# Attention loop of a fused transformer block: masked-query transposes moved to the first gap, attended transpose ahead of the weighted values, projection moved to the values' bank

## Chip, cores and metric

The kernel runs on 1 core of one Trainium2 chip. The metric is device time in microseconds of one execution, the median of the runs.

## What is computed

Two blocks follow each other on x of 16 sequences x 128 tokens x 128 features, all float32. The change touches the first, a conditioned transformer block:

```python
mod = (c @ ada_w.T + ada_b)[:, None, :]
sh_msa, sc_msa, g_msa, sh_mlp, sc_mlp, g_mlp = jnp.split(mod, 6, axis=-1)
h = modulate(rmsnorm(x, norm1_w), sh_msa, sc_msa)
qkv = (h @ qkv_w.T).reshape(B, N, 3, H, D)      # H = 16 heads of D = 8
q, k = rmsnorm of each head, then rotary positions
attn = softmax(einsum('bnhd,bmhd->bhnm', q, k) * D ** -0.5)
o = einsum('bhnm,bmhd->bnhd', attn, v).reshape(B, N, C)
x = x + g_msa * (o @ proj_w.T + proj_b)
ff = silu(h2 @ w1.T) * (h2 @ w3.T) @ w2.T       # h2 from x as h above
x = x + g_mlp * ff
```

(The two lines on q and k are abridged.) The second block is linear attention with two layer norms; it is not touched.

## The kernel before

Every engine runs its own instruction stream, written out by hand, and waits on semaphores; the order of the calls in each stream is the order of the work. All matrix results go to eight banks of PSUM of 128 partitions x 512 float32. The work runs one sequence at a time. After a prologue that loads and transposes weights, a loop of LAST_A = 18 iterations (line 2014 for TensorE, 1447 for ScalarE, 1729 for VectorE, 1227 for GpSimd) runs as a pipeline in which iteration t works on several sequences at once:

- TensorE `round_(t, 0)` and `round_(t, 1)` (lines 1862 to 1890) are two half rounds. Each has 4 matmuls of raw scores of sequence t + 2 (line 1878, to banks 0 and 1), from which VectorE takes the row maxima (`rowmax`, line 1601), and 8 of transposed scores of sequence t that have the maxima folded in (line 1887, to banks 2 and 3), which ScalarE exponentiates (`exp`, line 1302). The second half round waits for the maxima and the exponentials of the first, since it writes the same banks. VectorE seeds a reciprocal square root for two sequences at a time (`square_sums`, `seeds`, lines 1658 to 1673) in iterations of odd t.
- `projection(t - 2)` (line 1898) multiplies the attended values of sequence t - 2 by the output weights, to columns 384:512 of bank 5. VectorE multiplies that by the gate (x1g, line 1648) and adds the input (x1, line 1651), both in `after_attention`.
- `token_major(t - 1)` (line 1906) transposes the value sums of sequence t - 1, which ScalarE copied out of bank 6 (`summed`, line 1371), back into the other half of bank 6. From there VectorE takes the reciprocals (line 1612) and the product o (`attended`, line 1620).
- `queries_and_keys(t + 3)` (line 1911) transposes padded queries and keys to bank 4; VectorE spreads them (`keys_apart`, `queries`, lines 1630 and 1638). GpSimd made them (`normed`, line 1192) out of rotated and normed heads; it also adds a bias to the input (`input_biased`, line 1224), for which x1 waits.
- `input_turned(t + 6)` (line 1933) and `queries_keys_values(t + 6)` (line 1940) are the input transpose and the product to queries, keys and values of a later sequence; ScalarE makes the modulated input between them (line 1319) and copies behind them (lines 1336, 1344, 1355). Both end at t = 9.
- `queries_and_max(t + 1)` (line 1948, helper line 1911) transposes the queries that carry their row maximum as a ninth element, the masked queries, to columns 0:256 of bank 5; ScalarE copies them to qTm (line 1328), which the next half rounds read.
- `weighted_values(t, 0)` and `(t, 1)` (line 1965) are 8 small matmuls each over the exponentials, to columns 0:256 of bank 6. From t = B - 6 = 10 on, the first of them stands ahead of the masked-query transposes and the second behind.
- `attended(t - 1)` (line 1977) transposes o of sequence t - 1 to bank 5, and ScalarE copies it (line 1363) for the projection one iteration later.

The profile records a float32 matmul as two rows' worth of instructions and a transpose as one.

From t = 14 on, parts of the feed-forward block (`b_first`, `b_input`, `b_rest`, lines 863 to 875) are dealt into the iterations. At t = 10 to 13 TensorE prepares biases and centred weights in them, and VectorE has the style vectors (lines 1564 to 1568) at the end of t = 8. Behind the loop come the rest of the feed-forward block and the second block.

## Time and profile before

| | |
|---|---|
| median of 3 runs | 210.18 us (210.06, 210.18, 211.2) |
| span of the profiled execution | 208.4 us (its own time is not given apart from this) |
| TensorE matmul busy | 183.2 us (88%) |
| TensorE weight load busy | 143.4 us (69%) |
| VectorE busy | 165.3 us (79%) |
| ScalarE busy | 130.1 us (62%) |
| GpSimd busy | 140.7 us (67%) |
| attention loop, t = 0 to 15 | 29.3 to 128.9 us of the span |
| granted TensorE clock | full (2.4 GHz) in every slice |

The span goes from the first to the last recorded instruction of one execution; the runs are timed from outside and have a little more. Busy times are sums over instructions that can overlap on TensorE. In the rows further down, a start time is counted from the start of the span, and brackets give the idle time of the engine before the row with what released it.

### The profile page before, as it was taken

How to read it: one execution, taken by the hardware profiler on the slowest of the kernel's cores; microseconds unless marked ns; L12 is line 12 of the kernel's file. 1: busy time of each engine (PE TensorE's matmuls, PEld its weight loads, DVE VectorE, ACT ScalarE, POOL GpSimd, SP SyncE). 2: the span in 40 equal slices, each digit the busy share in tenths (PEclk: the TensorE clock that was granted, in tenths of full speed). 3: DMA queues.
4: the chain of work that ended last, by engine and by line, in shares of the span. 5: the costliest groups of instructions: out<-in, count | busy, mean ns of one | idle time of the engine just before them, and what ended most of it. 6: DMA issues, size and time to landing. Idle time of an engine off the chain costs nothing.

```text
span 208.4 us, 6070 instructions
## 1 busy us (share of the span) xinstructions
PE 183.2 (88%) x2039; PEld 143.4 (69%) x2039; DVE 165.3 (79%) x498; ACT 130.1 (62%) x377; POOL 140.7 (67%) x333
## 2 busy tenths in 40 slices
PE   2598887999899999898899899899998899999963
PEld 1355556677687777776677676799997677888642
DVE  6699898895979889996785615768889788999882
ACT  1367797666777777675545775445343367999741
POOL 8889798999888887958900583416443746768651
PEclk9999999999999999999999999999999999999999
DMA  6962007700000000000000000000000000000111
GB/s 113 282 207 113 0 9 288 318 2 3 3 3 2 6 3 0 3 0 5 3 0 3 3 0 2 3 0 2 5 0 0 2 3 0 0 28 28 50 50 53
DMA packets 10428, 8.32 MB, mean 40 GB/s; under 512 B 3105, under 2 KB 9886, under 8 KB 9886
## 3 DMA queue, kind: packets, MB, share of 16 engines
q1 hardware_dynamic: 7006, 7.25, 10.3%
q10 hardware_dynamic: 3392, 0.68, 1.6%
q8 instruction: 17, 0.28, 0.6%
q14 instruction: 13, 0.11, 0.2%
HBM read 6.86 MB, written 1.07 MB: 38 GB/s over the span
## 4 chain that ended last, share of the span: by engine, by line
PE 46%; DVE 16%; issue 6%; ACT 4%; POOL 3%; POOLq 0%; ACTq 0%; DVEq 0%
DVE qkpad L1601 6%; PE bank L1887 6%; PE bank L1965 5%; PE bank L1878 5%; PE bank L875 5%; PE bank L863 5%; PE bank L864 4%; PE bank L992 2%; PE bank L1940 2%; PE bank L908 2%; ACT probs L1302 1%; PE bank L1977 1%; PE bank L1911 1%; PE bank L972 1%; PE bank L1898 1%
## 5 line engine op out<-in xcount | busy, mean ns | idle before, releaser
L1601 DVE TENSOR_REDUCE qkpad<-bank 128x4 f32<-128x512 f32 x64 | 41.0, 683 | 12.1 <-PE bank L1878 11.0
L1302 ACT ACTIVATE probs<-bank 128x512 f32<-128x512 f32 x64 | 34.7, 594 | 22.3 <-PE bank L1887 22.3
L1887 PE MATMUL bank<-qTm,kBD 32*128 32x128 f32 x512 | 37.1, 283 | 0.4 <-ACT probs L1302 0.4
L1878 PE MATMUL bank<-kBD,qTs 32*128 32x256 f32 x224 | 31.8, 398 | 4.8 <-DVE qkpad L1601 3.7
L1887 PEld LDWEIGHTS bank<-qTm,kBD 32*128 32x128 f32 x512 | 31.0, 186 | 1.0 <-ACT probs L1302 0.6
L1878 PEld LDWEIGHTS bank<-kBD,qTs 32*128 32x128 f32 x224 | 20.0, 184 | 9.8 <-DVE qkpad L1601 6.6
L1965 PE MATMUL bank<-probs,vpad 128*32 128x128 f32 x512 | 18.5, 276 | 2.8 <-ACT probs L1302 1.6
L575 ACT ACTIVATE th<-bank 128x256 f32<-128x256 f32 x24 | 9.2, 383 | 18.7 <-PE bank L864 15.3
L1965 PEld LDWEIGHTS bank<-probs,vpad 128*32 128x32 f32 x512 | 12.8, 109 | 6.8 <-issue 3.1
L1911 PE MATMUL bank<-ident,qkpad 128*128 128x128 f32 x96 | 16.3, 279 | 0.4 <-POOL qkpad L1192 0.2
L1130 POOL TENSOR_TENSOR partner<-qk,rope 128x96 f32<-128x96 f32 x32 | 14.4, 470 | 3.2 <-ACT qk L1344 3.2
L1940 PE MATMUL bank<-qkvT,hT 128*128 128x384 f32 x32 | 15.3, 571 | 0.5 <-ACT hT L1319 0.5
L1911 PEld LDWEIGHTS bank<-ident,qkpad 128*128 128x128 f32 x96 | 11.2, 141 | 6.2 <-issue 3.1
L505 POOL TENSOR_TENSOR x<-fg,x 128x256 f32<-128x256 f32 x6 | 4.4, 727 | 15.5 <-DVE fg L691 15.5
L863 PE MATMUL bank<-hT,w1T 128*128 128x256 f32 x48 | 14.5, 384 | 0.0
L864 PE MATMUL bank<-hT,w3T 128*128 128x256 f32 x48 | 14.3, 379 | 0.0
L674 DVE SCALAR_TENSOR_TENSOR yg<-th,bank 128x256 f32<-128x256 f32 x24 | 10.0, 419 | 4.1 <-ACT th L575 4.1
L875 PE MATMUL bank<-w2T,ff 128*128 128x128 f32 x96 | 13.2, 275 | 0.0
L515 POOL TENSOR_TENSOR rstd<-var,minus_half 128x2 f32<-128x2 f32 (+1 forms) x17 | 11.7, 689 | 1.4
L875 PEld LDWEIGHTS bank<-w2T,ff 128*128 128x128 f32 x96 | 12.4, 191 | 0.4
L1141 POOL TENSOR_TENSOR rot<-qk,rope 128x256 f32<-128x256 f32 x16 | 11.7, 728 | 0.0
L1192 POOL TENSOR_TENSOR qkpad<-rot,ny 128x256 f32<-128x256 f32 x15 | 9.7, 647 | 2.2 <-DVE ny L1691 0.4
(253 smaller groups left out, 518.4 us busy)
## 6 DMA issues: line engine op xcount, KB each, us to landing
gate<-in_cond_dram SPq DMA_DIRECT2D x1, 1024.0 KB, 4.4
x<-gate_rows SPq DMA_DIRECT2D x1, 1024.0 KB, 4.6
y<-gate_rows SPq DMA_DIRECT2D x1, 1024.0 KB, 6.7
res<-gate_rows SPq DMA_DIRECT2D x1, 1024.0 KB, 10.1
out_dram<-res SPq DMA_DIRECT2D x7, 128.0 KB, 1.8
xin<-in_x_dram ACTq DMA_DIRECT2D x2, 256.0 KB, 5.3
xin<-in_x_dram SPq DMA_DIRECT2D x1, 512.0 KB, 5.0
ada_n<-in_L_cond_ada_w_dram SPq DMA_DIRECT2D x1, 256.0 KB, 5.3
```

Source lines behind the costliest of these rows:

```text
L515: q.tensor_tensor(rstd[:, rows], var[:, rows], minus_half[:, 0:rows.stop - rows.start], ALU.pow).then_inc(made, 1)
L863: q.matmul(bank[GU_BANK[c]][:, 0:UNIT * T], w1T[:, c * 128:c * 128 + 128], flat(hT2[1 - p]), start=True, stop=True)
L864: q.matmul(bank[GU_BANK[c]][:, UNIT * T:], w3T[:, c * 128:c * 128 + 128], flat(hT2[1 - p]), start=True, stop=True).then_inc(b_gu, 1)
L875: last = q.matmul(bank[F_BANK[j]][:, 0:D], ff[c][:, j * T:(j + 1) * T], w2T[:, c, :], start=c == 0, stop=c == FC - 1)
L1130: last = q.tensor_tensor(heads(partner[b % 2][:, :, :])[:, :, :, k::2], heads(qk[b % NQK][:, :, :])[:, :, :, 1 - k:ROPE:2], table(b, 1)[:, ...
L1302: q.activation(probs[2 * r + i][:, :, :, :].rearrange("p f a t -> p (f a t)"), bank[E_BANK[i]][:, :], ACT.Exp, scale=SCALE).then_inc(s_p, 1)
L1601: q.tensor_reduce(out_, score_bank(b, r, i)[:, :].rearrange("p (f a t) -> p f a t", f=2, a=2), X_AXIS, ALU.max, negate=True).then_inc(s_ma ...
L1878: last = q.matmul(bank[S_BANK[i]][:, f * 2 * T:(f + 1) * 2 * T], qTs[b % 2][rows, f, :], kBD[b % NKB][rows, f, :, :].rearrange("p a t -> p ...
L1887: last = q.matmul(bank[E_BANK[i]][:, (2 * f + k) * T:(2 * f + k + 1) * T], kBD[t % NKB][rows, f, k, :], qTm[t % 2][rows, f, :], start=True ...
L1911: last = q.transpose(dst[:, at_ + f * T:at_ + (f + 1) * T], qkpad[b % NKB][:, s, 8 * f:8 * f + 8, :].rearrange("p h d -> p (h d)"), ident[ ...
L1940: q.matmul(front_bank(b)[:, 128:512], hT[b % 2][:, :], qkvT[:, :], start=True, stop=True).then_inc(s_qkv, 1)
L1965: last = q.matmul(bank[O_BANK][32 * c:32 * c + 32, r * T:(r + 1) * T], vpad[b % NVP][:, col:col + VSTEP], probs[2 * r + i][:, f, k, :], st ...
```

## The change

Three things move, and the waits follow them. On TensorE the masked-query transposes of iteration t go from the stretch behind the second half round to the stretch behind the first, ahead of the queries and keys; ScalarE's copy of them goes ahead of the modulated input. The transpose of o goes from behind the weighted values to ahead of them (for t < B), and ScalarE's copy of it ahead of the squares; for t >= B - 6 the first weighted values no longer stand ahead of the masked queries. The projection writes columns 0:128 of bank 6, the values' bank, in place of bank 5. So it waits for the copy of the value sums, VectorE's gate multiplication waits for the transposes in that bank, and the next weighted values wait for the gate multiplication. On VectorE the reciprocals, the gate multiplication (now `gated_projection`) and o come right behind the first maxima, and the addition to x1 behind the second maxima.

```diff
@@ -957,5 +957,5 @@
                     e.wait_ge(c_hT, u + 1)
                     if u == 0:
-                        e.wait_ge(s_on, B)
+                        e.wait_ge(s_x1g, B)
                         e.wait_ge(pv_v, V_DONE)
                     wait(e, c_kx, u)
@@ -1454,13 +1454,16 @@
                 if t >= B - 2:
                     b_input(t - B, t % 2)
+                queries_and_max(t + 1)
                 modulated_input(t + 6)
                 exp(t, 1, 0)
                 exp(t, 1, 1)
-                queries_and_max(t + 1)
+                if t < B:
+                    attended(t - 1)
                 squares(t + 6)
                 queries_keys(t + 6)
                 if t >= B - 1:
                     b_rest(t - B)
-                attended(t - 1)
+                if t >= B:
+                    attended(t - 1)
                 summed(t)
                 values(t + 6)
@@ -1639,12 +1642,19 @@
                                 ALU.mult).then_inc(s_kq, 1)
 
-            def after_attention(b):
+            def gated_projection(b):
 
                 if not is_seq(b):
                     return
                 v.wait_ge(s_proj, b + 1)
+                v.wait_ge(s_oq, min(b + 2, B))
+                wait(v, s_x1, b)
                 if b == 0:
                     v.wait_ge(ld_g1, 16)
-                q.tensor_tensor(x1g[:, :], bank[P_BANK][:, 384:512], g1_rows[:, b, :], ALU.mult).then_inc(s_x1g, 1)
+                q.tensor_tensor(x1g[:, :], bank[O_BANK][:, 0:D], g1_rows[:, b, :], ALU.mult).then_inc(s_x1g, 1)
+
+            def after_attention(b):
+
+                if not is_seq(b):
+                    return
                 v.wait_ge(s_x1g, b + 1)
                 v.wait_ge(s_xb, b + 1)
@@ -1730,16 +1740,14 @@
                 rowmax(t + 2, 0, 0)
                 rowmax(t + 2, 0, 1)
-                if t < B:
-                    after_attention(t - 2)
                 reciprocals(t - 1)
+                gated_projection(t - 2)
+                attended(t - 1)
                 keys_apart(t + 3)
                 queries(t + 3)
-                attended(t - 1)
                 if t == B - 1:
                     b_first(t - B)
-                if t >= B:
-                    after_attention(t - 2)
                 rowmax(t + 2, 1, 0)
                 rowmax(t + 2, 1, 1)
+                after_attention(t - 2)
                 square_sums(t + 6)
                 seeds(t + 6)
@@ -1895,6 +1903,7 @@
                     return
                 e.wait_ge(s_oT, b + 1)
+                e.wait_ge(s_oT4, min(b + 2, B))
                 wait(e, s_x1g, b)
-                q.matmul(bank[P_BANK][:, 384:512], oT[:, :], projT[:, :], start=True, stop=True).then_inc(s_proj, 1)
+                q.matmul(bank[O_BANK][:, 0:D], oT[:, :], projT[:, :], start=True, stop=True).then_inc(s_proj, 1)
 
             def token_major(b):
@@ -1945,5 +1954,5 @@
                     return
                 e.wait_ge(s_max, NC * (b + 1))
-                wait(e, s_x1g, b - 2)
+                wait(e, s_oT, b - 2)
                 halves(bank[P_BANK], 0, b, 0).then_inc(s_tp, 1)
 
@@ -1956,4 +1965,5 @@
                     e.wait_ge(s_v, max(b + 1, FRONT_B))
                     wait(e, s_on, b)
+                    wait(e, s_x1g, b - 1)
                     if b == 0:
                         e.wait_ge(pv_a, A_ROWS)
@@ -1973,6 +1983,4 @@
                 e.wait_ge(s_on, b + 1)
                 wait(e, s_qTm, min(b + 3, B))
-                if b >= B - 2:
-                    e.wait_ge(s_x1g, b)
                 q.transpose(bank[P_BANK][:, 256:384], o[:, :, :].rearrange("p h d -> p (h d)"), ident[:, :]).then_inc(s_oTp, 1)
 
@@ -2014,11 +2022,14 @@
             for t in range(LAST_A):
                 round_(t, 0)
+                projection(t - 2)
+                token_major(t - 1)
                 if t == B - 1:
                     b_first(t - B, t % 2)
                     b_input(t - B, t % 2)
-                projection(t - 2)
-                token_major(t - 1)
                 if t >= B:
                     b_first(t - B, t % 2)
+                if t == 0:
+                    e.wait_ge(pv_a, A_DONE)
+                queries_and_max(t + 1)
                 queries_and_keys(t + 3)
                 input_turned(t + 6)
@@ -2031,11 +2042,7 @@
                 round_(t, 1)
                 queries_keys_values(t + 6)
-                if t >= B - 6:
-                    weighted_values(t, 0)
-                if t == 0:
-                    e.wait_ge(pv_a, A_DONE)
-                queries_and_max(t + 1)
-                if t < B - 6:
-                    weighted_values(t, 0)
+                if t < B:
+                    attended(t - 1)
+                weighted_values(t, 0)
                 if t == B - 1:
                     b_rest(t - B, t % 2)
@@ -2044,5 +2051,5 @@
                     b_input(t - B, t % 2)
                     b_rest(t - B, t % 2)
-                attended(t - 1)
+                    attended(t - 1)
             blocks_tensor(e, 2)
 
```

How this moves TensorE's instructions. Names are destination<-sources; each f32 matmul counts once here; `ident` marks a transpose. Before, iteration t = 3, from the end of the first half round (projection of line 1898, value transposes 1906, queries and keys 1911, input 1933):

```order
L1898 MATMUL bank<-projT,oT 128x128 [waits s_x1g,s_oT]
L1906 MATMUL bank<-ident,oT 128x128 [waits s_oT4]
L1906 MATMUL bank<-ident,oT 128x128
L1911 MATMUL bank<-ident,qkpad 128x128 [waits s_kq,s_nm]
L1911 MATMUL bank<-ident,qkpad 128x128 x3
L1933 MATMUL bank<-ident,xs 128x128 [waits s_v,s_xs]
```

and from the end of its second half round (1940 queries-keys-values, 1911 with s_x1g and s_max the masked queries, 1965 weighted values, 1977 transpose of o):

```order
L1911 MATMUL bank<-ident,qkpad 128x128 [waits s_x1g,s_max]
L1911 MATMUL bank<-ident,qkpad 128x128
L1965 MATMUL bank<-probs,vpad 32x128 [waits s_on,s_v,s_p]
L1965 MATMUL bank<-probs,vpad 32x128 x7
L1965 MATMUL bank<-probs,vpad 32x128 [waits s_p]
L1965 MATMUL bank<-probs,vpad 32x128 x7
L1977 MATMUL bank<-ident,o 128x128 [waits s_qTm,s_on]
```

The change, the same iteration (every line number is higher here; 1907 is the projection, 1915 the value transposes, 1920 the masked queries first and then queries and keys):

```order
L1907 MATMUL bank<-projT,oT 128x128 [waits s_x1g,s_oT4,s_oT]
L1915 MATMUL bank<-ident,oT 128x128 [waits s_oT4]
L1915 MATMUL bank<-ident,oT 128x128
L1920 MATMUL bank<-ident,qkpad 128x128 [waits s_oT,s_max]
L1920 MATMUL bank<-ident,qkpad 128x128
L1920 MATMUL bank<-ident,qkpad 128x128 [waits s_kq,s_nm]
L1920 MATMUL bank<-ident,qkpad 128x128 x3
L1942 MATMUL bank<-ident,xs 128x128 [waits s_v,s_xs]
```

and behind the second half round (1949 queries-keys-values, 1985 transpose of o, 1975 weighted values):

```order
L1949 MATMUL bank<-qkvT,hT 128x384 [waits s_hT]
L1985 MATMUL bank<-ident,o 128x128 [waits s_qTm,s_on]
L1975 MATMUL bank<-probs,vpad 32x128 [waits s_on,s_x1g,s_v,s_p]
L1975 MATMUL bank<-probs,vpad 32x128 x7
L1975 MATMUL bank<-probs,vpad 32x128 [waits s_p]
L1975 MATMUL bank<-probs,vpad 32x128 x7
L1886 MATMUL bank<-kBD,qTs 128x256 [waits s_qTm,s_p,s_max,s_kq]
```

The masked-query pair has gone into the upper stretch, the transpose of o stands ahead of the values, and the projection has a wait for s_oT4, the copy of the value sums, in the place where it stood.

VectorE in the same iteration, before, from the gate multiplication on (1648 x1g, 1651 x1, 1612 reciprocals, 1630 and 1638 keys and queries spread, 1620 o, 1601 second maxima, 1658 square sums):

```order
L1648 TENSOR_TENSOR x1g<-bank,x 128x128 [waits s_proj]
L1651 TENSOR_TENSOR x<-x1g,xin 128x128 [waits s_xb,s_x1g]
L1612 RECIPROCAL rsum<-bank 128x16 [waits s_oq]
L1630 TENSOR_TENSOR kBD<-bank,pmask 128x512 [waits s_e1,s_e0,s_tq]
L1638 TENSOR_SCALAR qTs<-bank,rowmask 128x256
L1620 TENSOR_TENSOR o<-bank,rsum 128x128 [waits s_oTp,s_rec]
L1601 TENSOR_REDUCE qkpad<-bank 128x2x2 [waits s_s0]
L1601 TENSOR_REDUCE qkpad<-bank 128x2x2 [waits s_s1]
L1658 TENSOR_REDUCE nms<-sq 128x32 [waits s_sq]
```

and with the change (1615 reciprocals, 1653 x1g, 1623 o, 1633 and 1641 keys and queries, 1604 second maxima, 1661 x1, 1668 square sums):

```order
L1615 RECIPROCAL rsum<-bank 128x16 [waits s_oq]
L1653 TENSOR_TENSOR x1g<-bank,x 128x128 [waits s_x1,s_oq,s_proj]
L1623 TENSOR_TENSOR o<-bank,rsum 128x128 [waits s_oTp,s_rec]
L1633 TENSOR_TENSOR kBD<-bank,pmask 128x512 [waits s_e1,s_e0,s_tq]
L1641 TENSOR_SCALAR qTs<-bank,rowmask 128x256
L1604 TENSOR_REDUCE qkpad<-bank 128x2x2 [waits s_s0]
L1604 TENSOR_REDUCE qkpad<-bank 128x2x2 [waits s_s1]
L1661 TENSOR_TENSOR x<-x1g,xin 128x128 [waits s_xb,s_x1g]
L1668 TENSOR_REDUCE nms<-sq 128x32 [waits s_sq]
```

o has moved from fifth to third place behind the first maxima, and x1 from ahead of the second maxima to behind them. GpSimd's and SyncE's orders are as before.

## Rows read from the trace of the kernel before

**Rows 1.** Waits of TensorE, whole span: total us, times, longest us.

```profile
PE bank L1878 <- DVE qkpad L1601: 3.7, 9, 1.3
...
PE bank L1898 <- ACT oT L1363: 0.9, 2, 0.5
```

**Rows 2.** Timeline, TensorE, iteration t = 8: start us, us, engine, line, operation.

```profile
78.44 0.48 PE L1878 MATMUL bank<-kBD,qTs 32*128 32x256 f32 x2
...
79.55 0.49 PE L1898 MATMUL bank<-projT,oT 128*128 128x128 f32 x2
79.87 0.38 PE L1906 MATMUL bank<-ident,oT 128*128 128x128 f32 x2
80.09 0.60 PE L1911 MATMUL bank<-ident,qkpad 128*128 128x128 f32 x4
...
81.00 0.48 PE L1878 MATMUL bank<-kBD,qTs 32*128 32x256 f32 x2 [0.20 <-DVE qkpad L1601]
...
82.85 0.38 PE L1911 MATMUL bank<-ident,qkpad 128*128 128x128 f32 x2
83.16 1.08 PE L1965 MATMUL bank<-probs,vpad 128*32 128x128 f32 x32
84.17 0.33 PE L1977 MATMUL bank<-ident,o 128*128 128x128 f32 x1
84.43 0.48 PE L1878 MATMUL bank<-kBD,qTs 32*128 32x256 f32 x2
```

**Rows 3.** Timeline, VectorE, t = 7 to 8.

```profile
79.27 0.20 DVE L1673 TENSOR_SCALAR ny<-nms 128x64 int32<-128x64 int32 x1
79.61 1.29 DVE L1601 TENSOR_REDUCE qkpad<-bank 128x4 f32<-128x512 f32 x2
...
81.13 0.42 DVE L1651 TENSOR_TENSOR x<-x1g,xin 128x128 f32<-128x128 f32 x1
81.47 0.24 DVE L1612 RECIPROCAL rsum<-bank 128x16 f32<-128x16 f32 x1
...
82.77 1.28 DVE L1601 TENSOR_REDUCE qkpad<-bank 128x4 f32<-128x512 f32 x2
```

**Rows 4.** Windows: length, busy us of PE, PEld, DVE, ACT, POOL; clock; DMA.

```profile
50.44:56.98 6.54, 5.86 (x95) 4.57 (x95) 5.63 (x14) 4.62 (x14) 6.04 (x15) 1.00 0.01 3
56.98:87.55 30.57, 29.02 (x471) 22.70 (x471) 27.29 (x66) 22.74 (x66) 25.94 (x63) 1.00 0.01 3
93.59:97.43 3.84, 3.06 (x60) 2.13 (x60) 2.96 (x8) 1.47 (x3) 3.23 (x9) 1.00 0.02 4
99.96:103.71 3.75, 3.02 (x62) 2.11 (x60) 2.95 (x8) 1.47 (x3) 3.26 (x8) 1.00 0.02 4
107.07:110.32 3.25, 2.94 (x60) 2.07 (x59) 2.20 (x5) 1.36 (x3) 0.00 (x0) 1.00 0.00 0
112.88:116.10 3.22, 2.95 (x59) 2.07 (x60) 2.90 (x10) 1.36 (x3) 0.00 (x0) 1.00 0.00 0
118.47:121.63 3.16, 2.93 (x51) 2.06 (x51) 0.86 (x3) 2.01 (x5) 2.85 (x6) 1.00 0.00 0
124.44:129.36 4.92, 4.55 (x58) 3.33 (x57) 3.23 (x10) 2.71 (x8) 2.45 (x5) 1.00 0.00 2
```

**Rows 5.** Timeline, ScalarE, t = 8.

```profile
78.72 0.38 ACT L1371 ACTIVATE oT<-bank 128x256 f32<-128x256 f32 x1
...
82.25 1.08 ACT L1302 ACTIVATE probs<-bank 128x512 f32<-128x512 f32 x2 [0.95 <-PE bank L1887]
```

**Rows 6.** Timeline, TensorE, queries and keys of t = 3.

```profile
49.74 0.66 PE L1911 MATMUL bank<-ident,qkpad 128*128 128x128 f32 x4 [0.24 <-POOL qkpad L1192]
```

**Rows 7.** Timeline, TensorE, weighted values of t = 3, 10 and 12.

```profile
53.16 1.08 PE L1965 MATMUL bank<-probs,vpad 128*32 128x128 f32 x32 [0.48 <-DVE o L1620]
...
95.53 0.64 PE L1965 MATMUL bank<-probs,vpad 128*32 128x128 f32 x16 [0.76 <-ACT probs L1302]
...
109.49 0.64 PE L1965 MATMUL bank<-probs,vpad 128*32 128x128 f32 x16 [0.30 <-ACT probs L1302]
```

More of the change, by code:

```diff
@@ L1644, in after_attention @@
                     return
-                v.wait_ge(s_proj, b + 1)
-                if b == 0:
-                    v.wait_ge(ld_g1, 16)
-                q.tensor_tensor(x1g[:, :], bank[P_BANK][:, 384:512], g1_rows[:, b, :], ALU.mult).then_inc(s_x1g, 1)
                 v.wait_ge(s_x1g, b + 1)
```

3 lines of the change are left out of this document (added).

## Prediction

> **What bounds the kernel now.** I read four views, in this order. The waits of TensorE come first: what did it stand still for? It waited for VectorE's row maxima nine times, 3.7 us in all, and twice for ScalarE before a projection, up to 0.5 us [rows 1]. The timeline of TensorE in one iteration of the attention loop, t = 8, comes second [rows 2]. The reader is to see two stretches. The first goes from the first half round (78.44) to the second (81.00), 2.56 us, and ends with 0.20 us of idle time released by the row maxima. The second goes from there to the next iteration (84.43), 3.43 us, with no idle time at all. Third, VectorE in the same iteration [rows 3]: the two maxima start at 79.61, end at 80.90, and the second half round follows 0.1 us later, so the first stretch is a chain (scores, maxima, scores) and not TensorE's own work. Last, windows of the loop [rows 4]: from the second half round of t = 4 to that of t = 9 TensorE is busy 29.02 of 30.57 us. So the first stretch is set by a chain through VectorE, the second by TensorE's instruction stream. Work that leaves the second and fits under the chain of the first is time saved.
>
> **Steady iterations, t = 4 to 9.** The pair of masked-query transposes moves from the second stretch to the first. Where it stands now it costs 83.16 - 82.85 = 0.31 us; the value transposes, the same kind of pair with transposes behind it, cost 80.09 - 79.87 = 0.22 us [rows 2]. The first stretch has 0.20 us idle, so a pair of 0.22 us fits to within 0.02: I take 2.56 us unchanged. Its bounds are 0 and +0.11 us (0.31 - 0.20). The transpose of the attended values goes ahead of the weighted values; it costs 84.43 - 84.17 = 0.26 us last in the stretch, and I expect 0.2 to 0.26 in its new place. The second stretch becomes 3.43 - 0.31 - 0.02 = 3.10 us. For that the weighted values must not wait: their first half needs exponentials of the first half round and the attended product o, which VectorE now makes third after the maxima instead of fifth, a microsecond earlier.
>
> ScalarE's moved copies cost nothing: the copy of the masked queries (0.38) goes into idle time of 0.95 us ahead of the exponentials [rows 5], and the copy of the attended values takes the place it left. If that cover were gone, TensorE would wait for the modulated input in front of the queries-keys-values product.
>
> VectorE sets the pace of every odd iteration, in which it also seeds the Newton steps. At t = 7 the seeds end at 79.47 and the maxima start at 79.61 [rows 3]: about 0.1 us of slack, in a period of 5.99. The change moves the addition to x1 (a step of 81.47 - 81.13 = 0.34) from before the second maxima to behind them. Its scores are there by then (1.1 us after the half round, against maxima that start at 1.77), so the maxima start 0.34 earlier and the seeds come out when they did. The sum of VectorE's steps is the same, but for a dependent pair (x1g, x1) that is pulled apart, perhaps 0.05. I take 5.85 us for an odd period and 2.56 + 3.10 = 5.66 for an even one, 0.47 less than 11.98 for a pair. From the second half round of t = 4 to that of t = 9 the window has 30.57 us [rows 4]: two pairs and one even period whose end the style work on VectorE sets. I get 5.66 + 5.85 + 5.66 + 5.85 + 6.50 = 29.52: **-1.05 us**.
>
> **Iterations 0 to 3.** At t = 3 TensorE waits 0.24 us for GpSimd's normed keys [rows 6], and GpSimd works without a pause until there. Whatever the first three iterations gain ends in that wait: **0 us** (were GpSimd not in the way, it would be 3 times 0.31). Behind it the gain begins: the weighted values of t = 3 wait 0.48 us for o [rows 7], since o stands behind x1, which waits for GpSimd. In the new order o no longer stands behind it. The window of 6.54 us from the second half round of t = 3 to that of t = 4 [rows 4] becomes an odd period like the others, 5.85: **-0.69 us**.
>
> **Iterations 10 to 14.** There is no projection to queries, keys and values any more. The first weighted values wait for o (0.76 us at t = 10, and about as long at t = 11; the view names ScalarE, whose exponentials end with o), and the transposes stand between the two halves of the values [rows 7]. In the new order the first half starts at once and the second waits for the last exponentials, 2.42 us after the half round (109.49 - 107.07). With 0.57 of values behind it the second stretch is 3.0 us. It is 3.84, 3.75, 3.25, 3.22 and 3.16 us at t = 10 to 14 [rows 4]; the last, which has 0.1 less in front of its values' wait, I take at 2.9. That saves 0.84 + 0.75 + 0.25 + 0.22 + 0.26 = 2.32 us. The second stretch of t = 9 saves 0.33 like the others. The first stretches pay 0.22 us for the moved pair at t = 10, 11 and 12, 0.1 at t = 13, where 0.1 is idle, and nothing at t = 14, where they wait for exponentials: 0.76. Together **-1.89 us**.
>
> **The last two iterations.** The attended transpose of t = 15 now comes ahead of 2 us of feed-forward work, +0.2; the projection behind it no longer waits for its copy but for the copy of the value sums, which was the next thing on ScalarE. 4.92 us [rows 4] become about 5.0: **+0.1**. Behind that, the same instructions run in the same order.
>
> **The sum.** -1.05 - 0.69 - 1.89 + 0.1 = -3.5 us. That is the end at which each piece finds its place with no new wait. The other end has 0.11 more in each first stretch from t = 4 on (ten of them, +1.1) and odd periods of 5.9 instead of 5.85 (+0.1): -2.3 us. Nothing in the rows favours either, so I take the middle, -2.9. The profiled execution has a span of 208.4 us; the median of the runs, 210.18, is 1.8 above it for what lies around the span, which the change leaves alone. So 205.5 for the span and **207.3 us** for the median. A difference of 0.5% (1.05 us) is about what a measurement of this kernel can tell from none.
>
> **A rule against the change.** The projection now writes the bank that already holds the value sums and their transposes. The rows show that the turns fit today: the copy of the sums starts at 78.72 and ends at 79.10 [rows 5], and the projection starts at 79.55 [rows 2]. The Trainium skill (PSUM — Partial Sum Buffer, section PSUM bank collisions raise a hardware error) says that accesses of different engines to one bank have to be kept apart by semaphores whatever their address. By that rule every user of this bank now takes turns, and if the turns were the bound the result would be that of the third rival below, 211.9 instead of 207.3. The rows above do not show such a bound.
>
> **Rivals.**
> *TensorE alone is the bound.* The moved pair costs the same wherever it stands, and only the shown idle time is to be had: 0.20 us in the six iterations 4 to 9, 1.2 us, while from t = 10 on the last exponentials give the pace as before. 209.0 us. For it: 29.02 busy of 30.57. Against it: the waits for o at t = 3, 10 and 11 are idle time of TensorE as well.
> *VectorE is the bound in odd iterations and gives the gain back.* If x1 ahead of the seeds is not paid for by earlier maxima, the seeds and the next maxima come 0.34 us late in three odd iterations (+1.0), and iteration 3 gains only half (+0.3): 2.9 - 1.3 = 1.6 us less than before, 208.6. For it: 0.1 us of slack. Against it: x1 leaves the path to the maxima by as much as it enters behind them.
> *The bank's turns block TensorE: slower.* The projection now waits for ScalarE's copy of the sums of the iteration before, and behind it stand the value transposes, the masked queries, the keys and the next half round. If it stood there 0.5 us, the longest wait in front of a projection [rows 1], each first stretch would grow by 0.45 and each second shrink by 0.33: +0.12 in 14 iterations, +1.7, **211.9 us**. It decides once the copy ends 1.5 us after the start of an iteration; it ends at 0.66 now. ScalarE has to run 0.8 us late, and nothing in its rows says so.
> *The change does less than it says:* the second stretch is refilled by ScalarE's last exponentials in every iteration. They end at 82.25 + 1.08 = 83.33, and the second half of the values would start at about 83.6: not before 0.2 us more is cut. 0 to 1 us of gain, 209.7.
>
> **How the numbers follow.** The forecast (206.4 to 208.2) has 0.68, and a gain above it 0.06; TensorE alone 0.08, VectorE 0.10, the refilled stretch 0.04, the turns 0.04. The rivals at 208.6 and 209.0 are faster by over 0.5% (the border is 209.13), the second only just. Faster: 0.68 + 0.06 + most of 0.18, less a little for waits nobody named, 0.83; same: 0.13; slower: 0.04. The range is 206.3 to 209.2: it takes in both ends of the sum, the gain of 3.5 and some more, and the first two rivals; beyond it lie the last two and the best case.
>
> **What would show it.** In the new profile, the first stretch of t = 8 should be 2.5 to 2.65 us with the maxima or nothing as releaser, the second 3.1; the idle time of TensorE before the second half round should be near 0 in even iterations and 0.1 to 0.2 in odd ones. GpSimd's keys should cost TensorE more than 0.24 us at t = 3 (some 0.7). The waits for o should be gone and waits for exponentials of 0.3 to 0.9 us should stand before the second values from t = 10 on. A wait for ScalarE before a projection of the loop, or periods of 6.0 in odd iterations, would prove me wrong.

## The result, and the profile of the changed kernel

| | before | changed |
|---|---|---|
| median of the runs | 210.12 us (4 runs) | 207.34 us (207.23 to 207.52, 4 runs) |
| ratio | | 0.9853, 95% interval 0.9829 to 0.9877 |
| span of the profiled execution | 208.4 us | 205.4 us |
| TensorE matmul busy | 183.2 us | 180.9 us |

Predicted were 207.3 and a span of 205.5. The interval of the ratio stays clear of 1, so the change makes the kernel 1.5% faster. The size is right; its parts are less so.

TensorE's waits in the changed kernel (total us, times, longest us), against [rows 1]. Line 1886 is the raw scores (1878 before), 1920 masked queries, queries and keys (1911), 1975 the weighted values (1965), 1907 the projection (1898).

```profile
PE bank L1886 <- DVE qkpad L1604: 3.4, 5, 1.2
...
PE bank L1975 <- ACT probs L1302: 2.0, 5, 0.5
...
PE bank L1920 <- POOL qkpad L1192: 1.1, 1, 1.1
...
PE bank L1907 <- ACT oT L1363: 0.5, 1, 0.5
```

The maxima release it five times instead of nine, but for almost as long in all; the exponentials hold the second half of the values five times (t = 10 to 14); GpSimd's keys hold it once, at t = 3, for 1.1 us instead of 0.24 [rows 6].

TensorE, t = 8, against [rows 2]:

```profile
76.86 0.48 PE L1886 MATMUL bank<-kBD,qTs 32*128 32x256 f32 x2
...
78.29 0.38 PE L1915 MATMUL bank<-ident,oT 128*128 128x128 f32 x2
78.51 0.82 PE L1920 MATMUL bank<-ident,qkpad 128*128 128x128 f32 x6
79.17 0.27 PE L1942 MATMUL bank<-ident,xs 128*128 128x128 f32 x1
79.53 0.48 PE L1886 MATMUL bank<-kBD,qTs 32*128 32x256 f32 x2
...
80.64 0.91 PE L1949 MATMUL bank<-qkvT,hT 128*128 128x384 f32 x2
81.39 0.27 PE L1985 MATMUL bank<-ident,o 128*128 128x128 f32 x1
81.59 1.08 PE L1975 MATMUL bank<-probs,vpad 128*32 128x128 f32 x32
82.60 0.48 PE L1886 MATMUL bank<-kBD,qTs 32*128 32x256 f32 x2
```

The six transposes stand together, and the second stretch is 82.60 - 79.53 = 3.07 us (3.43 before). VectorE around it, against [rows 3]; 1661 is the addition to x1, 1623 o:

```profile
64.66 0.83 DVE L1661 TENSOR_TENSOR x<-x1g,xin 128x128 f32<-128x128 f32 x1
...
78.19 1.28 DVE L1604 TENSOR_REDUCE qkpad<-bank 128x4 f32<-128x512 f32 x2
...
79.70 0.28 DVE L1623 TENSOR_TENSOR o<-bank,rsum 128x128 f32<-128x128 f32 x1
...
82.08 0.70 DVE L1661 TENSOR_TENSOR x<-x1g,xin 128x128 f32<-128x128 f32 x1
...
88.95 0.27 DVE L1661 TENSOR_TENSOR x<-x1g,xin 128x128 f32<-128x128 f32 x1
```

o starts 1.5 us after the first maxima. The three rows of line 1661 are t = 5, 8 and 9: the addition, behind the second maxima now, takes 0.83, 0.70 and 0.27 us for the same tile. Before, it took 0.65, 0.42 and 0.33 us in these iterations.

Windows, as in [rows 4]: from the second half round of t = 3 to that of t = 4, on to that of t = 9, and second stretches of t = 10 and 12.

```profile
50.45:56.53 6.08, 5.64 (x95) 4.45 (x94) 5.89 (x12) 4.80 (x14) 5.79 (x14) 1.00 0.01 3
56.53:86.39 29.86, 28.16 (x470) 22.32 (x470) 28.00 (x66) 22.03 (x66) 26.30 (x64) 1.00 0.01 3
92.29:95.28 2.99, 2.58 (x58) 1.87 (x58) 2.91 (x6) 1.25 (x3) 2.36 (x9) 1.00 0.03 8
...
104.68:107.67 2.99, 2.58 (x58) 1.87 (x57) 1.85 (x4) 1.25 (x3) 0.00 (x0) 1.00 0.03 5
```

| piece | before | changed | difference | predicted |
|---|---|---|---|---|
| to the second half round of t = 3 | 50.44 | 50.45 | 0.0 | 0 |
| to that of t = 4 | 6.54 | 6.08 | -0.46 | -0.69 |
| to that of t = 9 | 30.57 | 29.86 | -0.71 | -1.05 |
| to the projection of sequence 14 | 41.81 | 40.01 | -1.80 | -1.89 + 0.1 |
| to the end of the span | 79.0 | 79.0 | 0.0 | 0 |

Inside the fourth piece one second stretch is not like the others: that of t = 11 is 101.10 - 97.84 = 3.26 us, where t = 10 and 12 have 2.99.
Its raw scores begin and end like this, with a bias matmul (line 1843) among them:

```profile
97.84 0.48 PE L1886 MATMUL bank<-kBD,qTs 32*128 32x256 f32 x1
...
98.00 0.37 PE L1843 MATMUL bank<-bqv,ones 1*128 1x256 f32 x1
...
98.86 0.37 PE L1886 MATMUL bank<-kBD,qTs 32*128 32x256 f32 x1
```

### The profile page after: what moved, and what is told of

It is laid out like the page before. It is cut to its first block, busy times and chain, and to the rows that moved or that the text cites. A ratio compares the mean times of both kernels' runs of the same rounds, so it can differ in the third digit from the quotient of the medians.

```text
span 205.4 us, 6100 instructions
## 1 busy us (share of the span) xinstructions
PE 180.9 (88%) x2039; PEld 142.3 (69%) x2039; DVE 166.1 (81%) x498; ACT 129.4 (63%) x377; POOL 141.3 (69%) x333
## 3 DMA queue, kind: packets, MB, share of 16 engines
HBM read 6.86 MB, written 1.07 MB: 39 GB/s over the span
## 4 chain that ended last, share of the span: by engine, by line
PE 40%; DVE 17%; issue 8%; POOL 5%; ACT 4%; POOLq 0%; ACTq 0%; DVEq 0%
PE bank L1895 5%; DVE qkpad L1604 5%; PE bank L875 5%; PE bank L1886 5%; PE bank L863 5%; PE bank L864 4%; PE bank L1975 4%; ACT probs L1302 2%; PE bank L908 2%; POOL rstd L515 2%; PE bank L1907 1%; PE bank L1920 1%; PE bank L992 1%; PE bank L1949 1%; PE bank L972 1%
## 5 line engine op out<-in xcount | busy, mean ns | idle before, releaser
L1130 POOL TENSOR_TENSOR partner<-qk,rope 128x96 f32<-128x96 f32 x32 | 14.4, 471 | 2.0 <-ACT qk L1344 2.0
L1920 PE MATMUL bank<-ident,qkpad 128*128 128x128 f32 x96 | 14.2, 277 | 1.4 <-POOL qkpad L1192 1.1
L863 PE MATMUL bank<-hT,w1T 128*128 128x256 f32 x48 | 14.4, 382 | 0.0
```

The costliest lines, as they stand in the source:

```text
L863: q.matmul(bank[GU_BANK[c]][:, 0:UNIT * T], w1T[:, c * 128:c * 128 + 128], flat(hT2[1 - p]), start=True, stop=True)
L1130: last = q.tensor_tensor(heads(partner[b % 2][:, :, :])[:, :, :, k::2], heads(qk[b % NQK][:, :, :])[:, :, :, 1 - k:ROPE:2], table(b, 1)[:, ...
L1920: last = q.transpose(dst[:, at_ + f * T:at_ + (f + 1) * T], qkpad[b % NKB][:, s, 8 * f:8 * f + 8, :].rearrange("p h d -> p (h d)"), ident[ ...
```

## The experiments

The loop starts at 29.1 to 30.2 us in these profiles, whatever the kernel. In two of them (e5, e9) the granted clock was lower for a while after the loop, and in that of e7 on the kernel before it was lower ahead of the loop (0.50 in the window from 20 to 22 us). So beside the medians stands the **loop time**: from TensorE's first raw scores of t = 0 to its last projection, the one behind a 0.53 us wait. Before: 134.87 - 29.34 = 105.53 us; changed: 131.87 - 29.18 = 102.69. The medians of before that were taken beside the runs below lay between 210.18 and 210.59.

| kernel | median | loop time | against the changed kernel's loop |
|---|---|---|---|
| before | 210.12 | 105.53 | +2.84 |
| changed | 207.34 | 102.69 | |
| e1 TensorE's and ScalarE's orders back | 209.66 | 104.23 | +1.54 |
| e2 transpose of o last | 209.22 | 104.11 | +1.42 |
| e3 VectorE's order back | 207.99 | 102.99 | +0.30 |
| e4 projection in bank 5 | 220.62 | 115.16 | +12.47 |
| e5 x1 behind o | 206.91 | 101.99 | -0.70 |
| e6 x1 of t = 3, 5 put off | 207.03 | 102.36 | -0.33 |
| e7 no reciprocal square root | 206.62 | 101.45 | -1.24 |
| e7 the same on before | 209.32 | 104.75 | -0.78 against before |
| e8 biases in the wait | 207.35 | 102.42 | -0.27 |
| e9 e6 and squares first | 206.76 | 101.16 | -1.53 |
| e10 all together | 205.94 | 101.25 | -1.44 |
| e11 all together again | 205.76 | 101.10 | -1.59 |

The loop time by pieces, as in the table above, for the three kernels that undo an order (each piece ends at the second half round of the iteration named, the last two at the projections of sequences 14 and 15):

| kernel | t = 3 | t = 4 | t = 9 | projection 14 | projection 15 |
|---|---|---|---|---|---|
| before | 21.10 | 6.54 | 30.57 | 41.81 | 5.51 |
| changed | 21.27 | 6.08 | 29.86 | 40.01 | 5.47 |
| e1 | 21.08 | 6.08 | 30.53 | 41.06 | 5.48 |
| e2 | 21.08 | 6.08 | 29.85 | 41.63 | 5.47 |
| e3 | 21.23 | 6.50 | 29.72 | 40.07 | 5.47 |

**e1.** TensorE: masked queries ahead of the values and o last, as before; ScalarE likewise.

```diff
-                queries_and_max(t + 1)
                 queries_and_keys(t + 3)
...
+                queries_and_max(t + 1)
                 weighted_values(t, 0)
...
+                attended(t - 1)
```

> TensorE's and ScalarE's orders as before the change; VectorE's order and the projection in the values' bank stay as changed. Theory (the pair of transposes hidden under the maxima gives the steady gain, the earlier o gives the gain at t = 3, 10 and 11): the second stretch of t = 8 is again 3.35 to 3.45 us, the wait for o at t = 3 (0.48) and at t = 10 and 11 stays gone, and the time is 208.9 to 209.5 us. Rival (VectorE's new order makes the whole gain, since o comes earlier): 207.4 to 207.8. Rival (VectorE's order is worth nothing by itself): 210.1.

Measured: ratio to before 0.9959 (0.9925 to 0.9992). The second stretch of t = 8 is 83.60 - 80.17 = 3.43 us again, and the stretches of t = 10 and 11 stay at 3.25 and 3.30 (3.84 and 3.75 before), that of t = 3 at 3.43 (3.99). So VectorE's order, with the projection in its new bank, removes the waits for o and nothing else; the rival that gives it all the gain falls. About half of the change's loop time (1.54 of 2.84) is in the two orders. The median, 209.66, lies a little above the 208.9 to 209.5 expected; its runs go from 208.82 to 211.0, and the loop time alone would give 208.9.

**e2.** Only `attended(t - 1)` goes behind the weighted values again, on TensorE and ScalarE.

> Only the transpose of o and its copy go back behind the weighted values; the masked queries stay in the first stretch. Theory: in the steady iterations nothing changes (same instructions in the second stretch, 3.1 us), and from t = 10 on the transpose no longer fills 0.2 us of the wait for the last exponentials but stands behind it: +0.2 to 0.26 us in five iterations, 208.3 to 208.6. Rival (o ahead of the values holds them up when o is late, so that putting it last frees something): 207.3 or less.

Measured: 0.9933 (0.9903 to 0.9962), dearer than expected. The instructions of the second stretch are the same, as it says, but its time is not. TensorE, t = 8; 1946 is the product to queries, keys and values, 1982 the transpose of o:

```profile
79.72 0.48 PE L1883 MATMUL bank<-kBD,qTs 32*128 32x256 f32 x2
...
80.82 0.91 PE L1946 MATMUL bank<-qkvT,hT 128*128 128x384 f32 x2
81.67 1.09 PE L1972 MATMUL bank<-probs,vpad 128*32 128x128 f32 x32
82.69 0.33 PE L1982 MATMUL bank<-ident,o 128*128 128x128 f32 x1
82.94 0.48 PE L1883 MATMUL bank<-kBD,qTs 32*128 32x256 f32 x2
```

The same instructions take 3.22 us here and 3.07 in the changed kernel. The step of the product is 0.85 with the values behind it and 0.75 with a transpose behind it; the transpose's step is 0.25 behind the values and 0.20 ahead of them. I read this as the price of a change between full tiles and the 32-column tiles of the values, about 0.1 us by the first step; with the transpose behind the product there is one change less. No run isolates it.

The 0.15 us do not reach the time of the steady iterations, though: from the second half round of t = 4 to that of t = 9 this kernel takes 29.85 us and the changed one 29.86. The first stretches give back what the second ones cost (2.61 for 2.96 us at t = 6, 3.41 for 3.79 at t = 9), since VectorE sets the pace there. What e2 loses lies behind: its second stretches are 0.18 us longer at t = 9 and 0.25 to 0.26 at t = 10 to 14, and the last piece before the projection of sequence 14 is 0.14 longer, 1.6 us in all; 0.19 comes back in the first three iterations. So the expectation's 0.2 to 0.26 in five iterations holds, and 0.3 us come on top of it. And e1, which moves the masked queries back as well, is only 0.12 us slower than e2: they cost it 0.7 us in the steady iterations and give 0.6 back from t = 10 on, where they stood in the wait for the last exponentials.

**e3.** VectorE: gate multiplication, x1, reciprocals, keys, queries, o, second maxima.

> VectorE's order as before the change (gate multiplication, x1, reciprocals, keys, queries, o, second maxima); TensorE, ScalarE and the bank as changed. Theory: o ends 0.8 us later after the maxima, which in an even iteration is 0.2 to 0.3 us later than TensorE wants it (it asks for it 1.86 us after the second half round of t = 8 starts), and at t = 3 it waits for GpSimd's biased input as before (0.5); at t = 10 and 11 the values wait 0.8 again: 209.0 to 210.0 us, with rows of TensorE's transpose of o waiting for VectorE. The x1 addition behind the maxima's GpSimd-free moment goes back to 0.3 to 0.4 us and gives 0.1 to 0.3 us back per odd iteration, which is in this range. Rival (the order on VectorE does not matter, TensorE's stream alone does): 207.4.

Measured: 0.9880 (0.9849 to 0.9912), less than either end of what the theory gave. TensorE waits for o three times, 0.61 us at t = 3, 0.33 at t = 10 and 0.43 at t = 11, and the second stretches of t = 5 and 7 are 3.29 and 3.30 us where 3.07 stood:

```profile
51.22 0.47 DVE L1661 TENSOR_TENSOR x<-x1g,xin 128x128 f32<-128x128 f32 x1 [1.61 <-POOL xin L1224]
...
53.04 0.33 PE L1985 MATMUL bank<-ident,o 128*128 128x128 f32 x1 [0.61 <-DVE o L1623]
```

But the first stretches of t = 4, 6 and 8 fall from 3.02, 2.96 and 2.67 us to 2.60, 2.56 and 2.56. From the second half round of t = 4 to that of t = 9 this kernel needs 86.63 - 56.91 = 29.72 us, 0.14 less than the changed one. At t = 10 and 12 the second stretches are 2.99 and 3.00 us: the wait for the last exponentials hides a late o. VectorE's new order is worth 0.3 us in the loop: it gives 0.42 at t = 3, and in the steady iterations the first stretches of even iterations take 0.14 us more than the second ones of odd iterations give.

**e4.** The projection goes back to columns 384:512 of bank 5, and `queries_and_max` waits for `s_x1g`.

> The projection goes back to columns 384:512 of bank 5, everything else as changed; so the masked-query transposes, which write the same bank, wait for the gate multiplication on VectorE, which stands behind both first maxima. Theory (the move to the values' bank is what makes the place in the first stretch possible): TensorE stands at the pair for about 1.3 us in every iteration from t = 2 to 14, the keys, the input and the second half round behind it; the first stretch of t = 8 is 3.7 to 4.0 us in place of 2.67, and the time 220 to 227 us. Rival (the pair's wait is hidden under the maxima anyway, which the second half round waits for): the first stretch stays within 0.3 us, 208 to 211 us.

```profile
PE bank L1918 <- DVE x1g L1652: 14.4, 13, 1.6
```

Measured: 1.0477 (1.0429 to 1.0524); the first stretch of t = 8 is 86.16 - 82.35 = 3.81 us. Both are as the theory had them, and the rival falls. The move of the projection is what makes the place in the first stretch free. The loop grows by 12.5 us for 14.4 of waits.

**e5 and e6.** x1 elsewhere: right behind o in all iterations (e5), or that of t = 3 and 5 at the start of t = 4 and 6, with ScalarE's step behind it (e6; VectorE's part is shown):

```diff
+                if t in (4, 6):
+                    after_attention(t - 3)
                 reciprocals(t - 1)
...
-                after_attention(t - 2)
+                if t not in (3, 5):
+                    after_attention(t - 2)
```

> Only VectorE's addition to x1 moves: right behind o and ahead of the spread keys and queries, so ahead of the second maxima again. Theory (the addition takes 0.4 to 0.83 us behind the second maxima because GpSimd's operations with two inputs in SBUF run beside it, and 0.3 to 0.4 where it stood): where it stands now less of GpSimd's work meets it, the first stretches of t = 4 and 6 are 2.6 to 2.8 in place of 3.02 and 2.96 us, and the time is 206.8 to 207.3. Rival (VectorE is simply full in odd iterations, wherever the addition stands): 3.0 us as now, and 207.3 to 207.6, since the second maxima come late in even iterations as well.

> The additions to x1 of t = 3 and t = 5 (and ScalarE's step behind them) are put off to the next, even iteration, ahead of the reciprocals; all else as changed. Theory (in odd iterations addition, square sums and seeds behind the second maxima make the next maxima late): the first stretches of t = 4 and t = 6 fall from 3.02 and 2.96 to 2.55 to 2.65 us, and the time is 206.4 to 206.8. Rival (another chain ends at the same moment, GpSimd's keys or ScalarE's exponentials): the stretches fall by less than 0.2 and another releaser stands in front of the second half round; 207.1 to 207.4.

e5: 0.9834 (0.9802 to 0.9867), in the range of the theory. The first stretches of t = 4 and 6 are 2.53 and 2.52 us, though at t = 3 x1 waits 1.57 us for GpSimd's biased input and the second stretch is 3.56 instead. e6: 0.9832 (0.9807 to 0.9856), between theory and rival. At t = 6 the theory holds, 2.96 us becomes 2.56; at t = 4 the rival does, 3.02 becomes only 2.96. Without x1 the square sums of t = 3 wait for ScalarE's squares:

```profile
53.53 0.42 DVE L1671 TENSOR_REDUCE nms<-sq 128x32 f32<-128x256 f32 x1 [0.39 <-ACT sq L1336]
```

**e9.** On ScalarE the squares go ahead of the copy of o, on top of e6:

```diff
+                squares(t + 6)
                 if t < B:
                     attended(t - 1)
-                squares(t + 6)
```

> As the run with x1 put off, and on ScalarE the copy of the transpose of o goes behind the squares in place of ahead of them. There, at t = 3, VectorE's square sums waited 0.39 us for these squares, and the first stretch of t = 4 stayed at 2.96 us. Theory (exponentials, copy of o, squares, square sums, seeds, next maxima are one chain in an odd iteration, and the copy lies in it with 0.16 us): the first stretch of t = 4 falls to 2.75 to 2.85 and nothing else changes, 206.8 to 207.0. Rival (the copy hides, the seeds' own 0.63 us sets the end): 2.96 again.

Measured: 0.9820 (0.9787 to 0.9854). The first stretch of t = 4 is 2.57 us, more than was expected; and against "nothing else changes" that of t = 9 falls from 3.80 to 3.19 and that of t = 8 from 2.78 to 2.55, while that of t = 6 grows from 2.56 to 2.76. The loop is 1.2 us shorter than e6's for one copy, a step of 0.16 us, that changed places. VectorE behind the second maxima of t = 8, and GpSimd beside it, in e6:

```profile
82.01 0.71 DVE L1664 TENSOR_TENSOR x<-x1g,xin 128x128 f32<-128x128 f32 x1
...
82.97 0.39 DVE L1570 SCALAR_TENSOR_TENSOR csilu<-ctanh,condT 128x16 f32<-128x16 f32 x1
83.40 0.65 DVE L1571 TENSOR_SCALAR csilu<-csilu 128x16 f32<-128x16 f32 x1
...
81.99 0.58 POOL L1177 TENSOR_TENSOR rot<-rot,partner 128x192 f32<-128x192 f32 x1
```

and in e9:

```profile
81.14 0.40 DVE L1664 TENSOR_TENSOR x<-x1g,xin 128x128 f32<-128x128 f32 x1
...
81.80 0.21 DVE L1570 SCALAR_TENSOR_TENSOR csilu<-ctanh,condT 128x16 f32<-128x16 f32 x1
82.04 0.17 DVE L1571 TENSOR_SCALAR csilu<-csilu 128x16 f32<-128x16 f32 x1
...
81.08 0.32 POOL L1170 TENSOR_TENSOR ny<-ny,nt 128x64 f32<-128x64 f32 x1
```

Same instructions, same tiles. Where x1 starts with a long operation of GpSimd it ends when that has ended (81.99 + 0.58 = 82.57; x1 ends at 82.72). From the addition to the next maxima VectorE needs 85.00 - 82.01 = 2.99 us in e6 and 83.57 - 81.14 = 2.43 in e9. The traces divide t = 4's 0.39 in the same way. From the start of the second maxima of t = 3 to the next maxima it is 53.53 - 51.85 = 1.68 us to the square sums and 1.85 from there in e6, and 53.00 - 51.49 = 1.51 and 1.62 in e9. So the copy's place gives 0.17 us; the other 0.23 lies in VectorE's seeds, whose first operation takes 0.63 us in e6 and 0.20 in e9, while the second takes 0.38 and 0.61.

**e7.** GpSimd works without a pause in the first iterations, and one of its operations there takes 1.65 us: the reciprocal square root of the input norm for sequences 8 to 15. This kernel leaves it out and copies the argument:

```diff
-                    q.tensor_tensor(rstd_x[:, MID_B:], ms[:, MID_B:], minus_half[:, 0:B - MID_B], ALU.pow).then_inc(p_rstd, 1)
+                    q.tensor_copy(rstd_x[:, MID_B:], ms[:, MID_B:]).then_inc(p_rstd, 1)
```

> GpSimd's reciprocal square root for sequences 8 to 15 (1.65 us, in the iterations in which GpSimd works without a pause) is replaced by a copy of its input, about 0.2 us; the kernel leaves the reciprocal square root of the input norm out for these sequences, everything else as changed. Theory (what the first three iterations gain ends in the wait for GpSimd's keys at t = 3): that wait of 1.11 us is gone or under 0.2, and the time is 206.0 to 206.5. Rival (VectorE's or ScalarE's chain stands right behind GpSimd's): another wait takes its place, 207.0 to 207.4.

> The same edit (sequences 8 to 15 without the reciprocal square root of the input norm) on the kernel before the change. Theory: there GpSimd cost TensorE only 0.24 us at t = 3, and through x1 0.5 more in front of the weighted values; so it gains 0.3 to 0.8 us, 209.3 to 209.9, and the change is worth 0.4 to 0.8 us more than with the reciprocal square root (3.3 to 3.7 in place of 2.85). Rival (GpSimd does not take the first iterations' gain): both kernels gain the same, and the difference stays 2.8 to 3.0.

Measured: 0.9812 (0.9789 to 0.9834), and 0.9951 (0.9928 to 0.9974) on the kernel before; 206.62 us lies just above what was expected, 209.32 at the lower end. The wait for GpSimd at t = 3 is gone, and a wait of 0.36 us for the maxima stands at t = 2. By the loop time the change is worth 104.75 - 101.45 = 3.30 us without this operation and 2.84 with it; by the medians it is 2.70 and 2.78. So the theory rests on one profiled execution of each kernel here, and the medians, whose runs spread by 0.5 us and more, don't show it.

**e8.** `prepare_biases` and `prepare_centred` go between the two halves of the weighted values.

> TensorE's preparation of biases and centred weights at t = 10 to 13 moves from the first stretch into the wait for the last exponentials, between the two halves of the weighted values; all else as changed. Theory (from t = 10 on the second stretch is set by ScalarE's last exponentials and TensorE idles 0.41, 0.46, 0.41 and 0.41 us there, while the first stretch has no idle time at t = 10, 12): the waits shrink to 0 to 0.2 us, and what is saved in the first stretches (0.27 at t = 10, up to 1.0 at t = 12) comes out of the time: 206.0 to 206.6. Rival (the second stretch is full as well, the preparation is merely moved): 207.2 to 207.5.

Measured: 0.9845 (0.9814 to 0.9876), 207.35 us where 206.0 to 206.6 was expected; the time is the rival's. What fits the wait is won: the first stretches of t = 10 and 12 fall from 2.83 and 3.58 us to 2.55 and 2.55. But the second stretch of t = 12 grows from 2.99 to 3.70, and at t = 13 the centred weights, a step of 0.84, stand in a wait of 0.41, while the first stretch idles 0.52 without them:

```profile
110.34 0.48 PE L1886 MATMUL bank<-kBD,qTs 32*128 32x256 f32 x2 [0.52 <-DVE qkpad L1604]
...
112.28 0.91 PE L1855 MATMUL bank<-lin,centre 128*128 128x384 f32 x2
```

**e10 and e11.** What gained, in one kernel. The reciprocal square root is there, split in two parts of four columns. x1 stands behind o, but for the iterations named in the expectations.

> Everything that gained, in one kernel: x1 right behind o except at t = 3, where it is put off to t = 4; the copy of o behind the squares; the preparation of biases in the wait for the exponentials; GpSimd's reciprocal square root for sequences 8 to 15 in two parts of 4, the second ahead of the input of sequence 12. Theory (these are separate places: GpSimd's wait at t = 3 -0.8, odd iterations -0.7 to -1.0, t = 10 to 13 -1.0): 204.4 to 205.4 us. Rival (what one gives the next takes back, GpSimd working without a pause until t = 6): 206.0 to 206.8.

> The combination again, with x1 of t = 5 put off to t = 6 like that of t = 3 (in the combination before, x1 of t = 5 stood behind o and waited 1.16 us for GpSimd's biased input, which the second part of the reciprocal square root had made late; the second stretch of t = 5 was 4.32 us in place of 3.06), and x1 of t = 4 and 6 behind the second maxima. Theory: the stretch is 3.06 again and the first stretch of t = 6 stays under 2.8, so the loop ends 1.0 to 1.2 us earlier than in the combination before: 204.7 to 205.1 us. Rival (GpSimd's 1.03 us in that iteration come out at the keys of t = 6 in any case): 205.5 to 206.0, with a wait of TensorE for GpSimd at t = 6.

Measured: 0.9784 (0.9756 to 0.9812) and 0.9780 (0.9754 to 0.9807), both faster than the changed kernel by 1.4 to 1.6 us, and both above what was expected. By the loop time they add nothing to e9 (101.25 and 101.10 against 101.16 us), so what the pieces gain singly does not add up. Four columns of the reciprocal square root take 1.03 us, eight 1.65. The second four stand in GpSimd's stream at t = 5 (from 60.43 us in e10), its biased input comes later by them, and x1 waits for it where it stands right behind o, at t = 5 in e10 and at t = 7 in e11:

```profile
63.14 0.47 DVE L1667 TENSOR_TENSOR x<-x1g,xin 128x128 f32<-128x128 f32 x1 [1.16 <-POOL xin L1227]
```

```profile
73.49 0.46 DVE L1667 TENSOR_TENSOR x<-x1g,xin 128x128 f32<-128x128 f32 x1 [0.95 <-POOL xin L1227]
```

So e11's rival holds in the time (205.5 to 206.0) and in the kind of wait, but one iteration later than it was put. TensorE waits for GpSimd's keys at t = 7 too, 0.37 us.

## Why the prediction was right, and where it was not

**What holds is the mechanism.** Each second stretch loses the masked-query pair, the first stretch takes it up, and from t = 10 on the exponentials set the second stretch: e1 puts the pair back and the second stretch is 3.43 us again, e4 takes the bank away and the place in the first stretch is gone.

**Iterations 10 to 14** and the last two: -1.80 us measured, -1.79 predicted, by two errors that cancel. The second stretches of t = 10, 12 and 13 end with the last exponentials at 2.99 us, as predicted (3.0), and that of t = 14 is 2.91. But that of t = 11 is 3.26: a bias matmul (line 1843) runs among its scores, the last raw scores start 1.02 us after the half round in place of 0.75, and the last exponentials come later by as much. That is 0.26 us less gain than "3.75 becomes 3.0". The first stretches pay it back: t = 10 and 12 pay 0.22 each as predicted, but t = 11 pays 0.03 for 0.22 and t = 13 0.05 for 0.1. The reason given for t = 10 and 11, that o was late, was one of two: the pair ahead of the second values is the other. e1 removes the first by VectorE's order and e3 the second by TensorE's, and either alone takes most of the gain.

**The first three iterations** end in GpSimd's wait, as predicted (1.11 us; some 0.7 were named). Without the operation that e7 leaves out, the change is worth 0.46 us more in the loop.

**The second stretch** of the steady iterations: 3.07 us for 3.10, again by two errors that cancel. "3.43 - 0.31 - 0.02" took the pair at its step of 0.31. e2 shows that its leaving alone gives 0.21; the transpose of o ahead of the values gives another 0.15, for which the step had 0.02. By e2 that 0.15 is worth nothing in the time of these iterations.

**The periods that VectorE sets are where it failed:** the odd ones and that of the style vectors. The periods from second half round to second half round that end at t = 4 to 9 took 6.08, 5.62, 6.03, 5.62, 5.73 and 6.86 us, where 5.85, 5.66, 5.85, 5.66, 5.85 and 6.50 were predicted. The sum of the differences is 0.57 us, all by which the measured pieces (-2.97) lie behind the -3.53 of the sum. 0.36 of it is the last period alone, which was put at 6.50 without a working of its own. I had taken the middle between the two ends of the sum without a cause for it, so the hit at 207.3 owes that much to luck.

The term that was mis-sized is the addition to x1, taken at its step of 0.34 us from the old place. Behind the second maxima of t = 3, 5, 7 and 8 its step is 0.55, 0.75, 0.46 and 0.62 us. The gate multiplication pays some of that back: pulled apart from the addition, its step is 0.15 us where it was 0.31, and the prediction gave it "perhaps 0.05". Two things more show in these periods. At t = 3 the first operation of the seeds took 0.63 us, where it took 0.27 before the change:

```profile
53.81 0.63 DVE L1678 TENSOR_SCALAR ns<-nms 128x64 f32<-128x64 f32 x1
```

and e6 shows that the period ending at t = 4 stays at 6.02 us even without the addition, since the squares are the next chain. For the period ending at t = 6 e6 does show the addition in its new place as the cause: 5.62 us without it, 6.03 with it. Why these operations take longer at one time than at another is argued from GpSimd's rows in the last section; no run changes GpSimd's work beside them and nothing else.

By the prediction's own signs the odd periods fail: "periods of 6.0 in odd iterations" were to prove it wrong, and two of three were 6.08 and 6.03. The idle time before the second half round was put at 0 in even iterations and 0.1 to 0.2 in odd ones; it is 0.44 and 0.39 us at t = 4 and 6, and none is listed at t = 3, 5, 7 and 8. The late seeds of an odd iteration are paid in the next, even one.

The rival that VectorE gives the gain back names the right engine at more than twice the size, 1.3 us for 0.57, and knows nothing of the style's period; e3, e5 and e6 place it.

**ScalarE's moved copies "cost nothing"** does not hold once x1 is out of the way: exponentials, copy of o, squares, square sums, seeds and the next maxima are a chain in odd iterations, and by e9 the copy's place in it costs 0.17 us. In the changed kernel itself x1 covers it: at t = 3 the squares end at 53.26 us, and the square sums start behind the addition only at 53.37.

**TensorE alone as the bound** falls with e5, e6 and e9, which shorten the loop with TensorE's instructions untouched. **The bank's turns** block nothing that counts: no projection of a steady iteration waits. One at the end of the loop does, that of sequence 14:

```profile
126.40 0.46 PE L1907 MATMUL bank<-projT,oT 128*128 128x128 f32 x2 [0.55 <-issue]
```

The view names no releaser. ScalarE's copy of the value sums, which the new wait is for, ends at 125.91 + 0.38 = 126.29. Before the change this projection waited 0.37 us for its own copy, and the value transposes behind it need the copy of the sums in any case; the piece grew by 0.12 us, 0.1 predicted. What a bank shared the wrong way costs, e4 shows: 12.5 us. By the rule that the Trainium skill states (PSUM — Partial Sum Buffer, section PSUM bank collisions raise a hardware error) the pair has to wait there although the columns differ; what a kernel without that wait would do, no run here shows.

## What to carry to other kernels

Find the stretch in which an engine idles behind a chain, and look in the other stretches for work that may stand there; check first which bank or buffer it shares, since e4's 12.5 us hang on that and on no order. Then ask which engine sets the whole period: in e2 a second stretch longer by 0.15 us cost the steady iterations nothing. Price a moved VectorE operation that reads two SBUF tiles by what GpSimd runs at its new time, not by its duration in the old place. Put nothing in a wait that is longer than the wait.

## What the hardware did that was not expected

The durations of VectorE's addition to x1 and of o in the changed kernel (ns: minimum, median, maximum):

```profile
L1661 DVE TENSOR_TENSOR x<-x1g,xin x16: 274/454/832, 46.1 to 132.8; 128x128 f32<-128x128 f32 x16
...
L1623 DVE TENSOR_TENSOR o<-bank,rsum x16: 270/278/292, 38.0 to 127.4; 128x128 f32<-128x128 f32 x16
```

and of the addition in the kernel before:

```profile
L1651 DVE TENSOR_TENSOR x<-x1g,xin x16: 291/340/653, 44.4 to 135.8; 128x128 f32<-128x128 f32 x16
```

The addition reads two 128x128 SBUF tiles; it takes 0.27 us with GpSimd idle (88.95). At 64.66 in the changed kernel it runs into this operation:

```profile
64.61 0.73 POOL L1141 TENSOR_TENSOR rot<-qk,rope 128x256 f32<-128x256 f32 x1
```

which ends at 65.34; the addition ends at 65.49. At t = 14 a few hundredths of a microsecond decide: in the changed kernel GpSimd's conversion of line 478 starts at 115.83, the addition at 115.90, and it takes 0.58 us, to 0.14 after the conversion's end; in the kernel before, the addition starts at 118.11, the conversion only at 118.19, and the addition takes 0.29. o, which reads one operand from PSUM, hardly varies. The Trainium skill (SBUF — State Buffer, section Who interferes with whom) says that a VectorE instruction with two SBUF inputs contends with a GpSimd instruction that reads SBUF, and that the shared ports are held for a whole instruction. These ends agree: the addition ends 0.14 to 0.15 us behind GpSimd's operation where GpSimd started first, and takes its 0.29 where it started first itself. It says that one with a single SBUF input doesn't, outside the two-port modes; the 128x16 multiplication of line 1571 took 0.65 and 0.17 us and the first operation of the seeds, 128x64, 0.20 to 0.63, and whether they run in such a mode no run here tells.

The granted clock fell in the last 8 us of the profiled executions of e5 and e9. That stretch of e5, and of e6, where it did not fall:

```profile
198.00:206.00 8.00, 3.78 (x20) 2.57 (x19) 2.23 (x6) 0.84 (x3) 2.36 (x5) 0.79 0.13 39
```

```profile
198.00:206.00 8.00, 3.20 (x26) 2.25 (x24) 2.63 (x9) 1.44 (x4) 2.39 (x5) 1.00 0.18 51
```

e5 had left the loop 0.63 us earlier (131.17 against 131.80) and ended 0.5 us later, 205.8 against 205.3. From 200 to 202 us its granted clock was 0.50, the lower level (1.2 GHz), and in the 2 us before, in which it began to fall (0.83 on average), TensorE was busy 0.82 us. In e10 it was busy 0.82 us in the same 2 us and the clock stayed at 1.00, so these rows do not tell why it fell.
